# Row sums of the softmax from ScalarE in all tiles, and six small changes of order, in an attention and expert kernel

## What is computed

```python
xn = (x - mean(x)) / sqrt(var(x) + 1e-5)
q, k, v = xn @ Wq.T + bq, xn @ Wk.T + bk, xn @ Wv.T + bv
qk = q @ k.T
theta = 0.5 + 0.2 * sigmoid(qk) + 0.15 * tanh(qk) + 0.1 * relu(qk)
s = softmax(theta) @ v @ Wo.T + bo
e = argmax(xn @ Wr + br)
f = gelu(xn @ W1[e] + b1[e]) @ W2[e] + b2[e]
out = x + s * silu(f)
```

## Time and profile before

| | |
|---|---|
| median of 3 runs | 527.48 us (527.33 to 527.98) |
| the profiled execution, its own time | 527.64 us |
| its span, first to last instruction | 525.6 us |
| TensorE (PE) busy | 515.6 us, 98% |
| VectorE (DVE) busy | 402.6 us, 77% |
| ScalarE (ACT) busy | 344.6 us, 66% |
| GpSimd (POOL) busy | 195.8 us, 37% |
| granted TensorE clock | 1.00 throughout (the upper level, 2.4 GHz) |

### The profile page before, as it was taken

How to read it: one execution, slowest core, us unless ns; L and a number is a source line. 1 busy time by engine, 2 the same in 40 slices (tenths; PEclk the granted TensorE clock), 3 DMA queues, 4 the chain that set the end, 5 groups by cost and what they waited for, 6 DMA issues and landing times.

```text
span 525.6 us, 10829 instructions
## 1 busy us (share of the span) xinstructions
PE 515.6 (98%) x3773; PEld 484.3 (92%) x3773; DVE 402.6 (77%) x811; ACT 344.6 (66%) x633; POOL 195.8 (37%) x227
## 2 busy tenths in 40 slices
PE   7999999999999999999999989999999999999997
PEld 6899998899989999899999979998999989999997
DVE  5898689946578855598555688768999998867887
ACT  4789778437356733466343575899787786777884
POOL 3218419913112222222112222005676785342441
PEclk9999999999999999999999999999999999999999
DMA  8964720031635711247311421005233232211221
GB/s 266 344 225 176 285 81 1 2 120 32 230 123 151 255 55 41 61 133 237 112 40 40 136 70 42 21 22 190 62 99 113 71 114 87 62 44 49 60 71 51
DMA packets 40754, 57.49 MB, mean 109 GB/s; under 512 B 3654, under 2 KB 35788, under 8 KB 40156
## 3 DMA queue, kind: packets, MB, share of 16 engines
q1 hardware_dynamic: 35452, 46.02, 26.5%
q0 software_dynamic: 3488, 9.47, 6.4%
q10 hardware_dynamic: 1760, 1.32, 0.8%
HBM read 41.07 MB, written 17.56 MB: 112 GB/s over the span
## 4 chain that ended last, share of the span: by engine, by line
PE 86%; ACT 6%; DVE 5%; issue 1%; POOL 1%; DMA 1%; ACTq 0%; DVEq 0%
PE ps L899 26%; PE ps L901 25%; PE ps L900 25%; PE ps L1014 5%; DVE stats L1375 2%; PE ps L1193 1%; PE ps L1080 1%; ACT hid L763 1%; POOL xn_all L464 1%; DMA xn_all<-in_L_attn_x_dram 1%; PE ps L1070 1%; ACT relu_s L628 1%; ACT tanh_s L625 1%; ACT theta L624 1%; PE ps L1045 1%
## 5 line engine op out<-in xcount | busy, mean ns | idle before, releaser
L899 PE MATMUL ps<-v_hi,pT_hi 128*128 128x258 f32 x256 | 74.9, 293 | 0.2
L747 ACT ACTIVATE hid<-ps,b_now 128x256 f32<-128x256 f32 x128 | 53.7, 472 | 29.7 <-PE ps L901 28.8
L900 PE MATMUL ps<-v_lo,pT_hi 128*128 128x258 f32 x256 | 72.5, 283 | 0.0
L901 PE MATMUL ps<-v_hi,pT_lo 128*128 128x258 f32 x256 | 72.3, 282 | 0.0
L1430 DVE SCALAR_TENSOR_TENSOR theta<-tanh_s,theta 128x512 f32<-128x512 f32 x64 | 47.3, 739 | 23.5 <-ACT tanh_s L625 22.9
L899 PE MATMUL ps<-w_hi_even,hidT_h 128*128 128x256 f32 x200 | 58.5, 293 | 1.6 <-DVE hidT_l L1727 1.1
L636 ACT ACTIVATE theta<-theta,neg_max 128x512 f32<-128x512 f32 x64 | 43.0, 720 | 24.9 <-DVE neg_max L1436 24.6
L519 POOL COPY unit_token<-sorted_token 128x2 int32 x19 | 4.5, 238 | 142.9 <-PE ps L1193 142.9
L901 PE MATMUL ps<-w_hi_even,hidT_l 128*128 128x256 f32 x200 | 56.6, 283 | 0.0
L900 PE MATMUL ps<-w_lo_even,hidT_h 128*128 128x256 f32 x200 | 56.6, 283 | 0.0
L778 ACT ACTIVATE g_sb<-y_sb 128x512 f32<-128x512 f32 x20 | 12.6, 631 | 65.8 <-DVE y_sb L1742 65.8
(11 more groups left out here) (258 smaller groups left out, 1641.5 us busy)
## 6 DMA issues: line engine op xcount, KB each, us to landing
w_raw_odd<-in_L_ffn_W_dram SPq DMA_DIRECT2D x10, 1024.0 KB
w_raw_even<-in_L_ffn_W_dram SPq DMA_DIRECT2D x6, 1024.0 KB
sorted_g<-g_sb SPq DMA_DIRECT2D x20, 256.0 KB, 2.2
xn_rows<-xn_all SPq DMA_DIRECT2D x4, 1024.0 KB, 6.2
x_tile<-in_L_attn_x_dram SPq DMA_DIRECT2D x32, 128.0 KB, 2.2
out_dram<-g_tile SPq DMA_DIRECT2D x32, 128.0 KB, 1.7
xn_all<-in_L_attn_x_dram SPq DMA_DIRECT2D x3, 1024.0 KB, 12.4
kept_xT<-passing_xT SPq DMA_DIRECT2D x2, 1024.0 KB, 4.0
```

The lines of the kernel that those rows point to most:

```text
L747: last = nc.scalar.activation(hid[:, j % 2, c * UNIT:(c + 1) * UNIT], ps[:, HID_BANK + j, c * UNIT:(c + 1) * UNIT], ACT.Gelu, bias=b1_now[ ...
L899: mm(dst, a_hi, b_hi, start=first, stop=False)
L900: mm(dst, a_hi, b_lo, start=False, stop=False)
L901: return mm(dst, a_lo, b_hi, start=False, stop=last)
```

## The change

1. **Row sums.** v has 256 columns, `twos` is gone, and all exponentials write their row sum with `accum_out`. At the end of `transposed_parts(n)` VectorE adds the two halves and doubles them; `finish` takes the reciprocal of that, ahead of its wait for the products.
2. **Tile 10.** At n = 10 (TPB + 2) TensorE does `weighted(9)`, `transposes(10)`, `job(10)`, where it did transposes, job, weighted.
3. **Layer norm.** Of the first four tiles ScalarE normalizes tile 0 alone; tile 1 goes to VectorE, which had tile 2.
4. **Statistics.** Two of the row statistics stand ahead of the first half of `thetas(0)` and two behind it (before: two behind it); the block of 14 later is 12.
5. **G.** The four products of G stand together, and tiles 4 to 7 of batch 0 are routed behind them, where they alternated.
6. **Else.** In the first unit of an expert, ScalarE and VectorE use the else branch of the first test, where they had a second test.

```diff
-    VW = D + 2
...
-                                         accum_out=exp_sums[:, h:h + 1] if n == NT - 1 else None).then_inc(exp_done, 1)
+                                         accum_out=exp_sums[:, j % 2, h:h + 1]).then_inc(exp_done, 1)
...
-            normalize(range(2))
+            normalize(range(1))
...
-                with act.If(full < u0 + 1):
+                with act.Else():
...
-                    last = product(o_bank(n)[:, 0:VW], pT_hi[n % 2][:, i, :], pT_lo[n % 2][:, i, :],
+                    last = product(o_bank(n)[:, 0:D], pT_hi[n % 2][:, i, :], pT_lo[n % 2][:, i, :],
...
-                    if m == DC - 1 and ec == DC - 1:
-                        last.then_inc(G_done, 1)
-                    route_0(4 + 2 * m + ec)
+            last.then_inc(G_done, 1)
+            for t in range(4, TPB):
+                route_0(t)
...
+                elif n == TPB + 2:
+                    weighted(n - 1)
+                    transposes(n)
+                    job(n)
                 else:
                     pe.wait_ge(pT_ready, n * 2)
                     transposes(n)
...
+                if 1 in halves:
+                    dve.wait_ge(exp_done, n * 2 + 2)
+                    v.tensor_scalar(twice_sum[:, n % 2:n % 2 + 1], exp_sums[:, n % 2, 0:1], exp_sums[:, n % 2, 1:2], 2.0,
+                                    ALU.add, ALU.mult).then_inc(summed, 1)
 
             def finish(n):
+                dve.wait_ge(summed, n + 1)
+                v.reciprocal(rden[:, n % 2:n % 2 + 1], twice_sum[:, n % 2:n % 2 + 1]).then_inc(rden_ready, 1)
+                bank = o_bank(n)
+                dve.wait_ge(rden_ready, n + 1)
                 dve.wait_ge(pv_done, n + 1)
-                bank = o_bank(n)
-                v.reciprocal(rden[:, n % 2:n % 2 + 1], bank[:, D:D + 1]).then_inc(rden_ready, 1)
-                dve.wait_ge(rden_ready, n + 1)
...
-            normalize(range(2, 3))
+            normalize(range(1, 3))
...
-            thetas(0, [0])
             dve.wait_ge(x_in[2], 16)
             row_statistics(range(2 * TPB, 2 * TPB + 2))
+            thetas(0, [0])
+            row_statistics(range(2 * TPB + 2, 2 * TPB + 4))
...
-            row_statistics(range(2 * TPB + 2, 3 * TPB))
+            row_statistics(range(2 * TPB + 4, 3 * TPB))
```

More of the change, by code:

```diff
@@ L90, in block_attention_moe @@
         neg_max = sb("neg_max", [P, 2, 2])
-        rden, exp_sums = sb("rden", [P, 2]), sb("exp_sums", [P, 2])
+        rden, exp_sums, twice_sum = sb("rden", [P, 2]), sb("exp_sums", [P, 2, 2]), sb("twice_sum", [P, 2])
         xnT_hi, xnT_lo = [sb("xnT_hi", [P, DC, S], F32R)], [sb("xnT_lo", [P, DC, S], F32R)]
         u_hi, u_lo = [sb("u_hi", [P, DC, S], F32R)], [sb("u_lo", [P, DC, S], F32R)]
-        v_hi, v_lo = [sb("v_hi", [P, TPB, VW], F32R)], [sb("v_lo", [P, TPB, VW], F32R)]
+        v_hi, v_lo = [sb("v_hi", [P, TPB, D], F32R)], [sb("v_lo", [P, TPB, D], F32R)]
         own_xT = sb("own_xT", [P, DC, S])
@@ L111, in block_attention_moe @@
             for kept, name in ((v_hi, "v_hi_2"), (v_lo, "v_lo_2")):
-                kept.append(view(second_v, name, [P, TPB, VW], F32R))
+                kept.append(view(second_v, name, [P, TPB, D], F32R))
         w1_hi_odd, w1_lo_odd = sb("w1_hi_odd", [P, DC, H], F32R), sb("w1_lo_odd", [P, DC, H], F32R)
@@ L218, in block_attention_moe @@
         late_scaled, late_ready = sem("late_scaled"), sem("late_ready")
-        last_summed, last_offset, last_added, last_gated = sem("last_summed"), sem("last_offset"), sem("last_added"), sem("last_gated")
+        summed, last_offset, last_added, last_gated = sem("summed"), sem("last_offset"), sem("last_added"), sem("last_gated")
         block = ctx.enter_context(nc.Block())
@@ L1466, in finish @@
                                        ALU.mult, ALU.add).then_inc(half_s_ready, 1)
[L1468 to L1472, removed]
             v.memset(ones[:, :], 1.0)
-            twos(0)
             v.memset(onehot[:, :, 0:1].bitcast(F32), 0.0)
@@ L1760, in first_unit_of @@
                     low_w1(e, other, 0)
-                with dve.If(full < u + 1):
+                with dve.Else():
                     parts_half(u, beside=lambda: low_w1(e, other, 0))
@@ L1855, in _ @@
             gated(last_u)
-            twos(1)
             for n in range(TPB + 1, NT - 2):
@@ L1887, in _ @@
             v.tensor_tensor(x_last, x_last, offset, ALU.add).then_inc(last_added, 1)
[L1888 to L1891, removed]
+            dve.wait_ge(summed, NT)
+            v.reciprocal(rden[:, n % 2:n % 2 + 1], twice_sum[:, n % 2:n % 2 + 1]).then_inc(rden_ready, 1)
             dve.wait_ge(rden_ready, NT)
```

## The result

The changed kernel takes 531.79 us (median of 6 executions, 529.68 to 532.17), the kernel before 527.55 beside it: the ratio is 1.0075, 95% interval 1.0062 to 1.0089. It is 4.2 us slower. I had forecast 529.0 and a range up to 530.2, so the direction was right and the size was not. The profiled execution took 531.90 us, with a span of 529.6.

The account below looks back on a forecast made before the run. TensorE, busy 98% of the span, was taken as the bound, with a ScalarE chain from us 343 to 360. 2.09 - 0.64 + 0.15 - 0.13 = +1.47 gave 529.0 us, range 527.5 to 530.2.

Parts of the forecast that it names:

- Tile 10: TensorE's values of tile 9, put first, wait for tile 8's half_s_ready; scores(12) start at 367.08 instead of 364.99: +2.09 us.
- the sum from there: From tile 9's values at 361.83: 0.14 start, 2.88 values, 0.87 transposes, 1.36 job, 5.25 us to scores(12).
- ScalarE's sums elsewhere: 62 more accumulator reads, 6.2 us of ScalarE, and VectorE's 31 sums are covered by idle time: 0 for TensorE.
- rival (c): Cover of the exponentials too thin in eight tiles, of batch 0 or late: 1.6 more, 530.6 us; chance 0.07.
- Two columns fewer: 768 products of the values in 32 tiles go from 258 to 256 columns, 0.83 ns each: -0.64 us.
- Rival (d): Two columns fewer in the values are worth nothing: +2.11, 529.6 us; chance 0.64 together with the main case.
- The start: bias_cols copied later on VectorE, +0.1, and a later wait for GpSimd's normalized rows at 43.79: together +0.15 us.
- Else: ScalarE's second test at the one half unit, where TensorE waits for the copy behind it, falls away: -0.13 us.
- (a): Tile 9's values don't wait since tile 8 finishes early; the order gives -1.24, total 525.8 us; chance 0.08.

Follow-up runs that it names:

- e8_filled: The changed kernel with nine products of 512 columns, results unread, on TensorE ahead of the wait before tile 9's values: 530.04 us, ratio 1.0047.
- the two runs: The kernel before with only the row sums from ScalarE (528.75 us), and with only accum_out on all exponentials, sums unused, 258 columns kept (528.89 us).
- e1_order_back: The changed kernel with TensorE's old order at tile 10 (transposes, job, values of tile 9): 528.80 us, ratio 1.0024 to the kernel before.
- e4_finish_first: The changed kernel with VectorE's finish of tile 8 moved ahead of the low parts of tile 9: 527.96 us, ratio 1.0002 to the kernel before.
- e6_else_alone: The kernel before with only the else branch in the first units: 527.92 us against 527.76, ratio 1.0004.
- e9_order_finish_else: The kernel before with TensorE's new order at tile 10, VectorE's earlier finish of tile 8, and Else: 527.30 us against 527.44, ratio 0.9998.

## Why the prediction was wrong, step by step

- **Tile 10, right in mechanism and size, but not complete.** The prediction gave +2.09 from the last unit to scores(12). With the clock kept up (`e8_filled`) the trace shows 2.02. The wait ended 0.06 after half_s, as read, and ScalarE's reads moved it. What failed is the step "the sum from there": it prices 24 values at 0.120, transposes at 0.87 and the job at 0.226 a product, all at the clock of before, behind an idle time that the same paragraph had made 2.6 to 3.2 us long. The clock was at the lower level for thirteen of the 24 products, spaced by 0.20 to 0.21 (+1.20 against `e8_filled`), and for the first transposes behind them (+0.33). That is +1.53, the largest part of the missing 2.8 us.
- **ScalarE's sums elsewhere, wrong.** The prediction put them at nothing and gave rival (c), a thin cover in batch 0, a chance of 0.07. They cost 0.60 in batch 0, 0.28 on the way to job(17) in the changed kernel. The cover was read from a steady late tile and carried over to stretches with other work. By the difference between the two runs, more than half of what the row sums cost in batch 0 (0.38 of 0.64) comes with VectorE's part, which I had called free "under the same cover".
- **Two columns fewer, wrong in its working.** The forecast was -0.64 spread over all tiles. In the six tiles from 366 to 414 there is nothing: 24 values and 12 scores take 2.890 and 2.745 before, 2.877 and 2.753 after (medians of six). From tile 18 on it is 0.03 to 0.07 a tile, because before they take 2.914 and 2.774 there and after 2.878 and 2.754 (medians again). From 425 to the end the changed kernel wins 0.5, near the forecast sum by luck. Rival (d), two columns worth nothing, is borne out as a sum in the early tiles and not in the late ones. The 24 values became faster in both, by 0.013 and 0.036.
- **The start.** Forecast +0.15, in the trace +0.49 at the second turn and +0.28 in `e1_order_back`, with the same edits. L936 was to start at 10.2: it started at 10.57 in the first and at 10.25 in the second, where the products ahead of it were not slow, so the path by bias_cols was read rightly and the difference is another clock at the start, below. In `e4_finish_first` those products were not slow either and L936 still came at 10.51: VectorE began its statistics of x there at 5.48, where it was 5.22 in `e1_order_back`.
- **Else.** Forecast -0.13. At its place it gives 0.14 to 0.24 in the seven traces that have it, and in the time of `e6_else_alone` nothing.
- **The rivals.** (a), that the values do not wait, is what `e4_finish_first` nearly made true: its condition, tile 8 finished early enough, was read rightly, and the order as it was did not meet it. Its price was not: it gave the order -1.24, and with the early finish it is worth 0.42 (`e4_finish_first`) and 0.58 (`e9_order_finish_else`), since the values of tile 9 still wait 0.52 for their own low parts.

The parts of the changed trace add up: 0.49 start, -0.15 to scores(7), 0.60 batch 0, -0.28 to expert 7, 3.55 tile 10, 0.28 job(17), -0.48 behind it, 4.01 in all. The forecast's 1.47 is 2.54 less: 1.46 of that is tile 10 (3.55 against 2.09), 0.60 batch 0, 0.34 the start (0.49 against 0.15), 0.28 job(17), 0.16 the columns (0.48 against 0.64), and -0.30 the two small gains ahead of expert 7 (-0.15 and -0.28 against -0.13).

## What to carry to other kernels

A forecast stall of 2 to 3 us on TensorE may not be paid only once: the products behind it can run at the lower clock, which cost 1.1 to 1.6 us here, so price them at that level too, or keep TensorE busy through the wait. When an order on one engine is moved, move what releases it on the others as well; one line on VectorE was worth 3.8 us. An operation added "where its engine is idle" is free only in the stretches whose own rows show that idleness, and a consumer that starts 0.06 after its operand has no cover even if no wait is listed.

## What I had not expected of the hardware

- The clock falls after the idle time, 1.4 us into the next burst in the changed kernel and 1.6 us with the order alone, and after the same wait in some executions and not in others (two of six with 2.6 us, five of six with 2.9).
- At the start of the program the eight products of M are spaced by 0.22 or by 0.43 us, a factor of two. Between executions the number of slow ones differs. The granted clock reads 1.00 there, but a trace has no record of it before us 7.07 (before) or 8.86 (changed), and the view prints 1.00 where there is none. In the twelve traces the record begins between 6.09 and 9.15. In each of them the spacing is 0.43 ahead of that point and 0.22 behind it, with at most one value in between where the two meet. So the slow products look like the lower level, and the "1.00 throughout" of the kernel before holds from 7.07 on. From the timelines of TensorE before and after:

```profile
6.50 2.17 PE L910 MATMUL ps<-wk_raw,wq_raw 128*128 128x256 f32 x8
...
9.18 1.09 PE L926 MATMUL ps<-ident,xn_all 128*128 128x128 f32 x8 [0.35 <-ACT xn_all L568]
```

```profile
6.50 3.06 PE L909 MATMUL ps<-wk_raw,wq_raw 128*128 128x256 f32 x8
...
9.64 1.09 PE L925 MATMUL ps<-ident,xn_all 128*128 128x128 f32 x8
...
10.57 0.99 PE L936 MATMUL ps<-bias_cols,wk_raw 128*128 128x48 f32 x8
```

  The edit stands behind these products, so it isn't their cause; what sets the moment at which the clock rises is open. It makes single traces differ by some 0.3 us at the start.
- The same twelve products of 512 columns take 2.724 or 2.765 a tile from 366 to 414 (median 2.745) and 2.774 from 435 on in the kernel before, and 2.753 and 2.754 after the change. Why two columns in another product change their spacing was not tried.
